# Two mixture-of-experts stages: ScalarE copies raw weights behind the GELUs and the token copy, and SyncE issues rows, results and biases ahead of weights

## The reference, cut to what matters

```
flat = hidden.reshape(T, d)                                   # layer-normalised, T = 4096, d = 256
router_probs = softmax(flat @ router_w + router_b)            # E = 8
topk_probs, topk_idx = top_k(router_probs, 2)
weights = zeros_like(router_probs).at[arange(T)[:, None], topk_idx].add(topk_probs)
sh = gelu(flat @ sw1 + sb1)                                   # 256 -> 512
shared_out = sh @ sw2 + sb2                                   # 512 -> 256
h1 = gelu(einsum('td,edh->teh', flat, rw1) + rb1)             # each expert 256 -> 512
expert_out = einsum('teh,ehd->ted', h1, rw2) + rb2            # 512 -> 256
mixed = einsum('ted,te->td', expert_out, weights)
x = x + shared_out + mixed
```

## Time and profile before

| | |
|---|---|
| time, median of 3 runs | 4138.96 us (4134.91 to 4142.33) |
| span of the profiled execution | 4122.5 us |
| PE busy over the span | 88% |
| DVE, ACT, POOL busy over the span | 70%, 47%, 39% |
| mean granted TensorE clock | 0.951 |

### The profile page before, as it was taken

The page is one execution under the profiler, slowest core; times in us unless marked ns, Lnnn a source line. Parts: engine busy times, 40 slices in busy tenths (PEclk is TensorE's granted clock), DMA queues, the critical chain, the costliest instruction groups (busy, mean ns, idle before and its releaser), DMA issues. The chain is left out here.

```text
span 4122.5 us, 60134 instructions
## 1 busy us (share of the span) xinstructions
PE 3626.3 (88%) x19193; PEld 2601.5 (63%) x19256; DVE 2877.5 (70%) x5355; ACT 1924.7 (47%) x4079; POOL 1607.9 (39%) x1485
## 2 busy tenths in 40 slices
PE   4888877999599999998799869887899799999998
PEld 3555556888588888887788735444666455554666
DVE  5777656656566666645665568886888666776898
ACT  3565644344355555544344344443344465666332
POOL 3766726444465666633644321101002444441000
PEclk8999978999899999999899989999999999999999
DMA  5999902465100000001356410001201444441000
GB/s 135 302 259 269 307 23 84 151 194 162 59 16 19 19 19 19 16 4 35 100 167 180 148 48 21 21 11 23 40 0 39 91 101 109 102 114 27 11 16 16
DMA packets 228873, 358.33 MB, mean 87 GB/s; under 512 B 36482, under 2 KB 132850, under 8 KB 221810
## 3 DMA queue, kind: packets, MB, share of 16 engines
q1 hardware_dynamic: 204038, 265.38, 22.1%
q0 software_dynamic: 24544, 89.36, 8.9%
HBM read 173.82 MB, written 172.20 MB: 84 GB/s over the span
## 5 line engine op out<-in xcount | busy, mean ns | idle before, releaser
L2894 DVE TENSOR_REDUCE ab_nmx<-banks 128x1 f32<-128x512 f32 x512 | 329.0, 684 | 136.0 <-PE banks L2681 133.8
L2825 ACT ACTIVATE ab_pt<-banks 128x512 f32<-128x512 f32 x512 | 283.0, 600 | 163.9 <-PE banks L2691 154.9
L1736 POOL TENSOR_TENSOR lb_pq<-lb_pq,lb_rr 128x512 f32<-128x512 f32 x192 | 206.2, 1077 | 305.1 <-DVE lb_rr L1597 301.8
L1462 ACT ACTIVATE lb_pq<-banks,lb_nmx 128x256 f32<-128x256 f32 x384 | 178.5, 470 | 229.4 <-DVE lb_nmx L1592 226.2
L2691 PE MATMUL banks<-ab_qT,ab_kT 128*128 128x512 f32 x512 | 252.3, 497 | 5.7 <-ACT ab_pt L2825 5.7
L358 ACT ACTIVATE da_pt<-banks 128x512 f32<-128x512 f32 (+1 forms) x384 | 179.3, 537 | 124.9 <-PE banks L270 120.6
L1592 DVE TENSOR_REDUCE lb_nmx<-banks 128x2 f32<-128x512 f32 x192 | 131.1, 683 | 148.0 <-PE banks L1314 146.8
L2681 PE MATMUL banks<-ab_kT,ab_qT 128*128 128x512 f32 x512 | 208.1, 410 | 21.1 <-DVE ab_nmx L2894 14.6
L285 PE MATMUL banks<-da_pt,da_vx 128*64 128x512 f32 (+3 forms) x1024 | 165.0, 467 | 35.3 <-POOL da_pt L578 31.8
L2465 PE MATMUL banks<-w_f_dT,f_hT 128*128 128x256 f32 x768 | 178.1, 382 | 4.0 <-ACT f_hT L2511 4.0
L576 POOL TENSOR_TENSOR da_pt<-da_pt,w_da_tri 128x384 f32<-128x384 f32 x128 | 148.0, 1157 | 85.7 <-ACT da_pt L358 85.6
(11 more groups left out here) (538 smaller groups left out, 11146.5 us busy)
## 6 DMA issues: line engine op xcount, KB each, us to landing
moe_xs<-zero SPq DMA_DIRECT2D x71, 512.0 KB, 11.8
moe_ys<-zero SPq DMA_DIRECT2D x71, 512.0 KB, 11.8
moe_a_w_raw<-in_moe_w SPq DMA_DIRECT2D x48, 512.0 KB, 3.9
moe_b_w_raw<-in_moe_w SPq DMA_DIRECT2D x48, 512.0 KB, 4.0
da_spill<-da_hi SPq DMA_DIRECT2D x128, 128.0 KB, 2.4
ab_spill<-ab_hi SPq DMA_DIRECT2D x128, 128.0 KB, 2.4
ab_qT<-ab_spill POOLq DMA_DIRECT2D x32, 392.0 KB, 5.7
ab_kT<-ab_spill POOLq DMA_DIRECT2D x32, 392.0 KB, 5.3
```

The costliest lines, as they stand in the source:

```text
L1462: nc.scalar.activation(pq[:, n % RING, t, :], ps[:, S_BANK + n % 2, 2 * P * t:2 * P * t + 2 * P], ACT.Exp, bias=nmx[:, n % RING, t:t + 1], ...
L1736: nc.gpsimd.tensor_tensor(pq[:, n % RING, :, :], pq[:, n % RING, :, :], bcast(rr[:, n % RING, :], 2, 2 * P), ALU.mult).then_inc(s_p, 1)
L2825: nc.scalar.activation(pt[:, s % RING, :], ps[:, EXP_BANK + s % 3, :], ACT.Exp, scale=AB_D ** -0.5).then_inc(s_e, 1)
L2894: nc.vector.tensor_reduce(nmx[:, g % 2, col:col + 1], ps[:, MAX_BANK + n % 3, :], op=ALU.max, axis=AX.X, negate=True).then_inc(s_mx, 1)
```

## The change

Two orders of calls are altered, nothing is added or taken away.

On ACT, `high_w1` and `high_w2` move from the head of step i to a place behind `exponentials`, `hidden` and `copy_tokens`, ahead of `normalise_rows`. On SP, `load_x` moves from behind the weights to the head of the step, so that the step is now rows, result, `b2`, `w1` with `b1`, `w2`, and then the tables of the next stage. The orders of PE, DVE and POOL, all waits, all buffers and all sizes stay.

```diff
                 for i in range(-3, N + 1):
+                    if 0 <= i + 3 < N and items[i + 3][0] == "unit":
+                        load_x(i + 3)
                     if 0 <= i - 1 < N and items[i - 1][0] == "unit":
                         store_y(i - 1)
                     if i + 1 in load_of and loads[load_of[i + 1]][1] == i + 1:
@@ -804,8 +806,6 @@
                         load_w1(load_of[i + 3])
                     if i + 2 in load_of and loads[load_of[i + 2]][1] == i + 2:
                         load_w2(load_of[i + 2])
-                    if 0 <= i + 3 < N and items[i + 3][0] == "unit":
-                        load_x(i + 3)
                     if load_next and 0 <= i - tables_at < load_next[0]:
                         load_next[1](sp, i - tables_at)
@@ -942,16 +942,16 @@
                 for i in range(-3, N):
-                    if i + 2 in load_of and loads[load_of[i + 2]][1] == i + 2:
-                        high_w1(load_of[i + 2])
-                    if i + 1 in load_of and loads[load_of[i + 1]][1] == i + 1:
-                        high_w2(load_of[i + 1])
                     if i + 1 in routed:
                         exponentials(routed[i + 1])
                     if i + 1 in number:
                         hidden(i + 1)
                     if i + 2 in turned:
                         copy_tokens(i + 2)
+                    if i + 2 in load_of and loads[load_of[i + 2]][1] == i + 2:
+                        high_w1(load_of[i + 2])
+                    if i + 1 in load_of and loads[load_of[i + 1]][1] == i + 1:
+                        high_w2(load_of[i + 1])
                     if i + 3 in normal_no:
                         normalise_rows(i + 3)
```

## The result

| | before | changed |
|---|---|---|
| median | 4136.97 us (4134.91 to 4142.33, 4 runs) | 4304.15 us (4299.27 to 4308.54, 4 runs) |
| ratio, 95% interval | | 1.0403 (1.0389 to 1.0418) |
| span of the profiled execution | 4122.5 us | 4306.3 us |
| mean granted TensorE clock | 0.951 | 0.931 |

The change makes the kernel 4.0% slower, 167 us against the forecast 176, and the time of 4304 lies 11 us from the forecast 4315.

The account below looks back on a forecast made before the run. It took the loop GELU, SP, landing, ACT's copy, GELU to bound the kernel, with PE following. Longer turns (82 and 83 us) plus stage ends (11) gave +176 on 4139: 4315 us, range 4242 to 4365.

Parts of the forecast that it names:

- The loop of before: Units: GELU, SP, weight landing, ACT's copy, GELU set turns of 13.59 and 13.51 us; cutting it could gain 64 us.
- POOL's two subtractions enter the chain: Units: both weight subtractions, 4.83 us for the pair, now run between ACT's token copy and POOL's cast of the rows.
- The chain from the transposes to the next up: Units: serial work on ACT, POOL and DVE from the transposes' end to the next unit's first matmuls, 9.4 us.
- The pause lowers the clock: Units: PE stands still 3.8 us at most before each up; the lower clock after it costs 1.4 us a turn.
- a turn: Time from one unit's first up matmul to the next unit's: 15.9 us without clock loss, 17.3 us with it.
- The Trainium skill's loop: Rival on PE's clock: every turn has a pause and starts slow, turns of 17.6 us, 4329 us; no separate chance.
- SP's new order is hidden: SP's reordered loads: weights are wanted some 10 us after issue, landing takes about 5, so costed at nothing.
- The ends of a stage: Each experts stage: later start 3.5, hand-over to the units 0.7, last up's clock loss 1.4; 5.6 us a stage.
- the hand-over: Start of the units in a stage: the first up at 730.4 against 729.58, put at 0.7 us.
- The sum: Whole kernel: 82 and 83 us from the turns of the two stages plus 11 for the ends, +176 us.
- The 16 us: Whole kernel before: median 4138.96 less profiled span 4122.5, some 16 us taken to lie around the span.
- The faster rival: Units: PE becomes the bound at 12.1 us a turn if POOL's pair leaves the chain; 4083 us, chance 0.04.

Follow-up runs that it names:

- e3: Changed kernel with POOL's rows' cast ahead of both weight subtractions and the b2 semaphore made two: 4079.01 us, 0.9870 of the kernel before.
- e4: Changed kernel with POOL's rows' cast between the subtractions of w1 and w2: 4293.44 us, 1.0385 of the kernel before.
- e11: e4 with one added wait: in the units POOL starts the second subtraction only after DVE's low_x: 4131.85 us, 0.9983 of the kernel before.
- e6: Changed kernel with 8 useless matmuls behind each unit's down, in PE's pause: 4247.70 us, 1.0273 of the kernel before.
- e7: Changed kernel with 4 useless matmuls behind each unit's down, in PE's pause: 4293.90 us, 1.0397 of the kernel before.
- e1: Kernel before with ACT's half of the change alone, SP's order as before: 4297.99 us, 1.0391 of the kernel before.
- e10: e3 with SP's old order: 4254.02 us, 1.0289 of the kernel before.
- e2: Kernel before with SP's half of the change alone, ACT's order as before: 4151.99 us, 1.0040 of the kernel before.
- e8: Changed kernel with ACT's copy of w1 back at the head of the step, w2's left behind the token copy: 4148.37 us, 1.0039 of before.
- e9: e8 with POOL's rows' cast between the two subtractions and the b2 semaphore made two: 4085.88 us, 0.9887 of the kernel before.

## Why the prediction was right, step by step

- **The loop of before is cut.** Right: the waits of ACT for w2 are gone.
- **POOL's two subtractions enter the chain.** Right, and shown by e3, e4 and e11, which only change what POOL does around the cast. The chain from the transposes to the next up was put at 9.4 us and measured 9.17; POOL's pair takes 4.75 in place of 4.83. The cast took 1.05, the value for an idle DVE.
- **The pause lowers the clock.** Right, and shown by e6. The Trainium skill's loop (TensorE: Matmul & The Clock Gate, HAM oscillation) in which every turn starts at the low clock is what the profile shows: 42 of the 44 turns are 17.1 us or longer, all but the first of each stage. The price was put at 1.4 us a turn, as part of the lower level might fall inside the pause; that part is 0.1 us, and the price measured 1.6 (the 1.7 us that a clock of 0.90 takes, less that 0.1). Without the clock a turn was put at 15.9 and is 15.7 us, as the first turn of either stage shows. The two errors, 0.2 us too long and 0.2 too short, cancel: 17.3 forecast, 17.24 and 17.30 measured. That it came out as close as this is luck. The reasoning that the price falls between 0 and 2.5 with the pause's length was not right; e7 shows a step.
- **SP's new order is hidden.** Right for the change (e1 and the full change differ by 6 us, within what the two comparisons leave open), but the reason given was only half: e10 shows that this order has a worth of 175 us once POOL makes the rows first, and e2, e8 and e9 that it delays the first unit where ACT's copy of w1 stands ahead of the GELUs.
- **The ends of a stage**, 5.6 us: from each stage's start (the issue of its first w1 on SP) to its first unit it was 169.6 and 169.3 us and is 175.4 and 173.8, 5.8 and 4.6 more against the 4.2 forecast (its 0.7 for the hand-over is 0.8 by its own figures, 730.4 against 729.58); the last down ends 18.6 us after the last up's start where it was 17.2, 1.4 as forecast.
- **The sum**: 22 x 3.65 + 7.2 = 87 and 22 x 3.79 + 6.0 = 89 us, 176 us in the two stages; 7 us more lie between the two profiled executions outside them, and the medians differ by 167. The 16 us that the text before took to lie around a span are not that: in the changed kernel a run of 4308.1 us has a span of 4306.3, so 1.8 us lie around it. By this, as an estimate, the profiled execution of before took 4124 us, 13 less than the median, and the comparison of the two spans makes the loss look larger than the medians do.
- **The faster rival** (PE the bound at 12.1, POOL's pair out of the chain) did not happen, but its condition was the right one: e3 meets it with 12.3 us a turn and 4079 us, against 4083 worked out for it.

## What to carry to other kernels

When an instruction is moved back on one engine, look at the other engine's instruction that waits for it, and at all that stands behind that one in its order: these move back too, even if they were ready. Orders on several engines that feed each other have to be changed together: here ACT's change alone is 3.9% slower, POOL's alone 5.5% slower, both 2.9% slower, and with SP's as the third 1.3% faster. And a pause of PE in a loop is worth counting twice, once as time and once as clock, as e6 shows, where useless matmuls in the pause made the kernel 56 us faster.

## What the runs showed of the hardware

- One added semaphore wait on POOL made the kernel 3.8% faster (4293.4 to 4131.9 us): a POOL subtraction that starts 0.08 us ahead of DVE's makes DVE's last 3.35 us in place of 1.23, and the longer pause of PE that follows brings the clock down as well (0.90 in the units of e4, 1.00 in those of e11).
- The clock after a single pause pays all or nothing: PE pauses of 3.4 and 3.2 us in each turn cost about 1.6 us of it a turn and pauses of 2.5 us about 1.4, while pauses of 1.6 and 1.1 us in each turn cost nothing. Between 1.8 and 2.5 us both were seen: e8's one pause of 1.8 us was followed by the lower level, one of 2.4 us in e10 was not, and in the kernel before, pauses of 2.1 to 2.3 us in the routed items stayed without it three times and were followed by it twice, where the expectation for e7 names only those that did not.
